# Layer 3's expert feed-forward in lanes of 32 rows, four experts to a round, with biases by a one-hot product, and one register load for all lanes

## The reference

```python
def _L3_ffn_ref(x, Wg, W1, b1, W2, b2):
    ...
    probs = jax.nn.softmax(logits, axis=-1)
    top1_val = probs.max(axis=-1).reshape(bt)
    top1_idx = probs.argmax(axis=-1).reshape(bt)
    masked = jnp.where(top1_idx[None, :] == jnp.arange(n)[:, None], top1_val[None, :], -jnp.inf)
    vals, idx = jax.lax.top_k(masked, cap)
    ...
    h = jax.nn.gelu(jnp.einsum('ncd,ndh->nch', xe, W1) + b1[:, None, :])
    out = jnp.einsum('nch,nhd->ncd', h, W2) + b2[:, None, :]
    ...  # tokens that were not kept stay as they are
```

## Time and profile before

| | |
|---|---|
| median of 3 runs | 1657.29 us (1657.05 to 1662.76) |
| the profiled execution | 1651.5 us, its span from first to last instruction 1649.8 us |
| TensorE busy over the span | 1462.4 us, 89% |
| VectorE, ScalarE, GpSimd busy | 60%, 40%, 26% |
| layer 0's lane rounds | from about 100 to 290 us of the span |
| layer 3's tiles | first up product at 1470.0, last `add_b2` at 1630.3 us |
| from there to the end | 19.5 us |

### The profile page before, as it was taken

How to read it: one execution, slowest core, us unless ns; L and a number is a source line. 1 busy time by engine, 2 the same in 40 slices (tenths; PEclk the granted TensorE clock), 3 DMA queues, 4 the chain that set the end, 5 groups by cost and what they waited for, 6 DMA issues and landing times. The chain is left out here.

```text
span 1649.8 us, 25908 instructions
## 1 busy us (share of the span) xinstructions
PE 1462.4 (89%) x8350; PEld 1109.7 (67%) x8350; DVE 983.9 (60%) x1754; ACT 657.0 (40%) x977; POOL 428.0 (26%) x366
## 2 busy tenths in 40 slices
PE   7997888765999999898999999999988999759994
PEld 5752333533787788687888888888877877536663
DVE  5666767335644364835777777775657433557665
ACT  3366767212233333324655555554333233211110
POOL 0602222000434410010333333332003443023331
PEclk9999999755999999999999999999998999859997
DMA  5348981652232240240220222210403332455743
GB/s 176 113 171 325 358 330 54 223 165 103 90 103 90 94 157 1 89 179 4 100 103 27 103 103 103 103 30 14 144 7 138 112 103 84 145 196 186 242 138 121
DMA packets 82919, 211.38 MB, mean 128 GB/s; under 512 B 10786, under 2 KB 57763, under 8 KB 74595
## 3 DMA queue, kind: packets, MB, share of 16 engines
q1 hardware_dynamic: 66944, 166.40, 28.2%
q0 software_dynamic: 15840, 43.27, 7.7%
q10 hardware_dynamic: 2, 0.00, 0.0%
HBM read 165.21 MB, written 44.43 MB: 127 GB/s over the span
## 5 line engine op out<-in xcount | busy, mean ns | idle before, releaser
L657 POOL DMA_INDIRECT results<-sb_big,sb_s_out_row x63 | 134.0, 2127 | 462.5 <-ACT sb_big L888 298.5
L962 DVE TENSOR_TENSOR sb_h_split<-sb_big,sb_h_split 128x2048 fp32r<-128x2048 f32 x78 | 178.5, 2289 | 87.1 <-ACT sb_h_split L957 87.1
L957 ACT CAST sb_h_split<-sb_big 128x2048 fp32r x78 | 146.6, 1903 | 34.1 <-issue 32.9
L853 PE MATMUL ps<-sb_big,sb_e_hT 128*128 x624 | 141.0, 379 | 1.1 <-DVE sb_e_hT L1010 1.1
L1102 DVE COPY sb_g_space<-sb_big 128x1024 f32 x168 | 107.9, 698 | 48.8 <-DMA sb_big<-in_l_routed 23.2
L320 PE MATMUL ps<-sb_h_split 128*128 128x512 f32 x312 | 133.3, 427 | 3.8 <-issue 2.8
L1102 ACT COPY sb_g_space<-sb_big 128x1024 f32 x120 | 118.5, 1046 | 40.7 <-DMA sb_big<-in_l_routed 21.7
L853 PEld LDWEIGHTS ps<-sb_big,sb_e_hT 128*128 128x128 f32 x624 | 118.2, 190 | 18.5 <-issue 1.3
L322 PE MATMUL ps<-sb_h_split 128*128 128x512 f32 x312 | 123.9, 397 | 0.0
L1503 POOL DMA_INDIRECT sorted_in<-sb_big,sb_p_slots x64 | 70.1, 1095 | 206.0 <-DVE sb_p_slots L1328 163.4
L321 PE MATMUL ps<-sb_h_split 128*128 128x512 f32 x312 | 123.4, 395 | 0.0
(11 more groups left out here) (450 smaller groups left out, 3180.5 us busy)
## 6 DMA issues: line engine op xcount, KB each, us to landing
sb_big<-in_l_routed SPq DMA_DIRECT2D x32, 1024.0 KB, 7.2
sb_big<-in_l2f_routed SPq DMA_DIRECT2D x8, 3072.0 KB, 10.6
sb_e_wring<-in_l_experts SPq DMA_DIRECT2D x16, 1408.0 KB, 6.8
sb_big<-in_l_routed SPq DMA_DIRECT2D x32, 512.0 KB, 7.4
sb_big<-results SPq DMA_DIRECT2D x32, 512.0 KB, 7.2
sb_big<-sorted_in SPq DMA_DIRECT2D x18, 512.0 KB, 4.2
by_token<-sb_big SPq DMA_DIRECT2D x12, 512.0 KB, 3.7
sorted_in<-sb_l1p_zero SPq DMA_DIRECT2D x2, 2048.0 KB, 9.6
```

Source lines behind the costliest of these rows:

```text
L657: pool.indirect_dma_start(out=results, out_offset=bass.IndirectOffsetOnAxis(ap=places.out_row[:, j:j + 1], axis=0), in_=self.tile(j), in_o ...
L853: last = pe.matmul(psum[:, 7, 0:D], self.hT[:, f // TPC, f % TPC * P:(f % TPC + 1) * P], self.weight(place, 2 * KD * self.F + f * D, D), s ...
L957: act.copy(self.own[part][:, 0, :], self.raw(e, part)).then_inc(self.own_high[part], 1)
L962: dve.tensor_tensor(self.own[part][:, 1, :], self.raw(e, part), self.own[part][:, 0, :], ALU.subtract).then_inc(self.own_low[part], 1)
```

## The change

Layer 3's feed-forward goes over to lanes. An expert gets units of 32 rows, so the most there can be are 4 * 16 + 15 = 79 units, in 20 rounds of four (`ROUNDS3`). With these inputs 72 of the 80 lanes hold tokens. A round does the following:

- ScalarE and VectorE copy two lanes' `W1` each to `own_up` (`fill_up`), and the four lanes' `W2` to `own_down` (`fill_down`: in even rounds three by ScalarE and one by VectorE, in odd ones two each). Both places hold one round, so a fill waits for the product of the round before.
- TensorE first multiplies a one-hot matrix `which` (16 experts x 128 rows, made once from the lanes' experts) with the biases of all experts, as a high and a low part in the type fp32r, and adds the lanes' products on top in the same bank (`add_bias`, `up_product`, `down_product`). ScalarE's gelu reads that bank, and ScalarE writes the down product's result (`result`). `add_b1` and `add_b2` are gone.
- TensorE reads no registers. ScalarE and VectorE read the round's four experts with one register load of four values.
- The 26 bits are spread over 20 rounds: one in an odd round and two in an even one (`tally_at`). `rank_even`, `choose_kept` and all of `add_dropped` come behind the last round.
- An expert's weights are 1 MB in two loads of 512 KB, each with a ring of four.

Layer 0's `experts_of` also loads all four numbers at once, on both engines. The diff, cut (removed lines that stand in the print above are mostly left out, and so are the waits and names that repeat):

```diff
+ROUNDS3 = -(-(LANES0 * NT + E3 - 1) // LANES0)
...
             def experts_of(self, eng, r, lanes):
-                return {g: eng.value_load(self.tile_expert[0:1, r * self.lanes + g:r * self.lanes + g + 1],
-                                          min_val=0, max_val=self.NE - 1) for g in lanes}
+                _, found = nc.values_load_multi_w_load_instructions(
+                    self.tile_expert[0:1, r * self.lanes:(r + 1) * self.lanes], engines=[eng.engine],
+                    min_val=0, max_val=self.NE - 1)
+                return dict(enumerate(found))
...
+            tally_at, n = {}, 0
+            for r in range(1, rounds):
+                for spot in range(2 - r % 2):
+                    if n <= TOP_BIT:
+                        tally_at[r, spot] = n
+                        n += 1
...
+                places = Slots("s3", own, route, runs0[:, 0:E, :], rounds, big[:, EXTRA:EXTRA + NT * D], None, LANES)
...
+                own_up = big[:, FCOL2:FCOL2 + LANES * UP].rearrange("p (g n) -> p g n", g=LANES)
+                own_down = big[:, EXTRA:EXTRA + LANES * DOWN].rearrange("p (g n) -> p g n", g=LANES)
+                ring_up = sb("e3_ring_up", [P, LANES, UP], on=own)
+                ring_down = sb("e3_ring_down", [P, LANES, DOWN], on=own)
+                bias = sb("e3_bias", [E, FU + D], on=own)
+                bias_high, bias_low = (sb("e3_" + n, [E, FU + D], F32R, on=own) for n in ("bias_high", "bias_low"))
+                expert_wide = sb("e3_expert_wide", [P, E], on=own)
+                which = sb("e3_which", [E, rounds * LANES, W], F32R, on=own)
...
+                def load_up(sp, e):
+                    if e >= 2:
+                        sp.wait_ge(up_in[e % 2], 16 * (e // 2) + e % 2)
+                    if e >= LANES:
+                        wait_last_round(sp, e - LANES, act_up, dve_up)
+                    sp.dma_start(ring_up[:, e % LANES, :], a["l3_experts"][e][:, 0:UP]).then_inc(up_in[e % 2], 16)
...
+                        for e in range(E + LANES - 1):
+                            if e < E:
+                                load_up(sp, e)
+                            if e >= LANES - 1:
+                                load_down(sp, e - LANES + 1)
+                            if e == LANES - 1:
+                                places.wait_known(sp)
...
+                        def tell_experts():
+                            pe.wait_ge(widened, 1)
+                            pe.matmul(psum[0:E, 5, 0:rounds * LANES], expert_wide[:], ident[:, 0:rounds * LANES],
+                                      start=True, stop=True).then_inc(told, 1)
+                        def add_bias(to, r, lo, n):
+                            lanes = which[:, r * LANES:(r + 1) * LANES, :].rearrange("e g w -> e (g w)")
+                            pe.matmul(to, lanes, bias_high[:, lo:lo + n], start=True, stop=False)
+                            pe.matmul(to, lanes, bias_low[:, lo:lo + n], start=False, stop=False)
+                        def up_product(r):
+                            if r >= 2:
+                                pe.wait_ge(raw, r - 1)
+                            add_bias(psum[:, r % 2, :], r, 0, FU)
+                            pe.wait_ge(rows_c, r + 1)
+                            pe.wait_ge(act_up, r + 1)
+                            pe.wait_ge(dve_up, r + 1)
                             for k in range(KD):
+                                for g in range(LANES):
+                                    lo = k * P + g * W
+                                    last = pe.matmul(psum[g * W:(g + 1) * W, r % 2, :], rT[:, r % 2, lo:lo + W],
+                                                     own_up[:, g, k * FU:(k + 1) * FU], start=False, stop=(k == KD - 1))
...
+                            pe.wait_ge(chosen, 1 if r == 0 else 2)
+                            up_product(r)
+                            if (r, 0) in tally_at:
+                                sum_tally(tally_at[r, 0])
+                            if r >= 1:
+                                turn_hidden(r - 1)
+                            if r + 1 < rounds:
+                                turn_rows(r + 1)
+                            if r >= 1:
+                                down_product(r - 1)
+                            if (r, 1) in tally_at:
+                                sum_tally(tally_at[r, 1])
+                        turn_hidden(rounds - 1)
+                        down_product(rounds - 1)
+                        sum_surely()
...
+                            wait_landed(act, down_in, experts[3])
+                            for g in range(1 + r % 2, LANES):
+                                last = act.copy(own_down[:, g, :], from_ring(ring_down, experts[g]))
...
+                        for r in range(rounds):
+                            now = experts
+                            if r + 1 < rounds:
+                                experts = experts_of(act, r + 1)
+                                fill_up(r + 1, experts)
+                                turned_rows(r + 1)
+                            act.wait_ge(up, r + 1)
+                            if r >= 2:
+                                act.wait_ge(hid_t, r - 1)
+                            act.activation(h[:, r % 2, :], psum[:, r % 2, :], ACT.Gelu_apprx_tanh).then_inc(raw, 1)
+                            if r >= 1:
+                                result(r - 1)
+                            if r == 0:
+                                act.wait_ge(places.traced, 1)
+                            fill_down(r, now)
+                        result(rounds - 1)
...
+                        def fill_up(r, experts):
+                            if r >= 1:
+                                dve.wait_ge(up, r)
+                            wait_landed(dve, up_in, experts[1])
+                            for g in (0, 1):
+                                last = dve.tensor_copy(own_up[:, g, :], from_ring(ring_up, experts[g]))
+                            last.then_inc(dve_up, 1)
+                        def fill_down(r, experts):
+                            if r >= 1:
+                                dve.wait_ge(down, r)
+                            wait_landed(dve, down_in, experts[r % 2])
+                            for g in range(1 + r % 2):
+                                last = dve.tensor_copy(own_down[:, g, :], from_ring(ring_down, experts[g]))
...
+                            told_rows = psum[0:E, 5, lo:hi].unsqueeze(2).to_broadcast([E, hi - lo, W])
+                            dve.tensor_scalar(which[:, lo:hi, :], told_rows, tile_rows[0:E, 0:1], None, ALU.is_equal
+                                              ).then_inc(chosen, 1)
...
+                        dve.tensor_tensor(bias_low[:], bias[:], bias_high[:], ALU.subtract).then_inc(bias_l, 1)
+                        choose_lanes(0, 0, LANES)
+                        experts = experts_of(dve, 0)
+                        fill_up(0, experts)
+                        choose_lanes(1, LANES, rounds * LANES)
+                        fill_down(0, experts)
...
+                        for r in range(rounds):
+                            now = experts
+                            if r >= 1:
+                                turned_hidden(r - 1)
+                            if r + 1 < rounds:
+                                experts = experts_of(dve, r + 1)
+                                fill_up(r + 1, experts)
+                            if (r, 0) in tally_at:
+                                try_bit(tally_at[r, 0] + 1)
+                            if r >= 1:
+                                fill_down(r, now)
+                            if (r, 1) in tally_at:
+                                try_bit(tally_at[r, 1] + 1)
+                        turned_hidden(rounds - 1)
+                        rank_even()
+                        choose_kept()
+                        add_dropped(0, NT)
```

227 lines of the change are left out of this document (102 added, 125 removed).

## The result

| | before | after |
|---|---|---|
| median of 8 runs | 1657.36 us (1653.24 to 1662.76) | 1665.60 us (1664.81 to 1668.77) |
| the profiled execution | 1651.5 us, span 1649.8 | 1665.1 us, span 1663.4 |
| TensorE, VectorE, ScalarE busy | 89%, 60%, 40% | 87%, 60%, 45% |
| layer 3's part, from the gate's product (L336) to the end | 210.8 us | 216.1 us |

The change makes the kernel slower, by 8.2 us or 0.5% by the two medians. The ratio of all executions is 1.0061, with a 95% interval of 1.0048 to 1.0075, which is 10 us. The forecast was no change.

A forecast was written before the change was run, and what follows sets the result against it. The prediction took TensorE to bound layer 3's tiles before and a chain through VectorE the new rounds. Layer 3 +1.3, layer 0 -4 and clock +2 made about -1 us, rounded to no change: 1657 us, range 1641 to 1677.

The forecast's parts named there:

- the chain through VectorE: Layer 3's rounds: VectorE's copy, load, fills and bits with TensorE's hand-overs set 15.7 us per two rounds, 7.85 a round.
- rival 4: Layer 3: full-width bias matmuls keep lanes from running beside each other, raising TensorE's 5.2 us; chance 0.04, shared with anything else slow.
- rival 3: Layer 3's register load costs like four single ones, 2.1 us: +0.9 in each of 19 rounds, 1672 us; chance 0.06.
- first up product, against that of before: Start of layer 3's loop: about 0.6 us later, for one more operation, low biases, a lane choice and a fill ahead.
- first two rounds: Layer 3's first two rounds run at the lower clock and take 15.2 us.
- eight pairs, chain alone: Layer 3's middle rounds: eight pairs of an even and an odd round at 15.7 us each, 126 us.
- drops of the clock: TensorE in layer 3: occasional drops after even rounds' gaps of about 2.3 us, two at 1 us each, +2.
- nineteenth round: Layer 3's nineteenth round takes 6.4 us, its bit being the last and half a one.
- last up product to the final additions: Layer 3's end, 1618 to 1639.0 us: last products, ranking, choosing and 16 `add_dropped` of 6.6 us in all.
- from there to the end: Final additions to the kernel's end: stores no longer decide, and the 0.2 us once waited there is saved.
- rival 1: Layer 3: gaps halve TensorE's clock again and again, a pair grows from 15.7 to 17.5 us, 1673 us; chance 0.23.
- Layer 0: Layer 0's lane rounds: shorter register loads give -2 in the last six rounds, -2 under the saturated DMA queue, sum -4.

The follow-up runs named there:

- The filler: Changed kernel plus 18 transposes of 128x128, result unread, before the second sum of each even round in layer 3; 0.9963 of the kernel before.
- layer 0 alone: Kernel before with only the change's layer 0 part, the lanes' experts read by one register load of four; 0.9985, on another chip 1.0000.
- the first group: Runs on one chip beside the kernel before: layer 0's part only 0.9985, layer 3's part only 1.0031, changed kernel with one bit 0.9837, with gap transposes 0.9963.
- the second group: Another chip: changed kernel 1.0063; with four single register loads 1.0261; with gap transposes plus rows off first 1.0012, or plus transposes ahead of first rounds 1.0017.

## Why the prediction was wrong

**The mechanism was right.** The two waits for weights are gone, TensorE no longer bounds the rounds, and the chain through VectorE gives the gain back. The up products alternate by 8.9 and 6.2 us (forecast 9 and 6.8), the undisturbed pair is 15.05 us (15.7), VectorE is idle 1.3 us ahead of the fills (1.0), TensorE 2.3 to 2.5 us ahead of each second sum (2.3). Without the bits the rounds are the 6 us that were named as their sign. Four lanes' products take 1.92 us, so rival 4 is out. The bias products take some 1.1 us a round (0.70 forecast); those of the up product, 0.66 for 0.46, are on the chain. The load of four with its arithmetic is 1.45 us of VectorE's queue (1.1 to 1.2 forecast, and just under the 1.5 that was named as rival 3's sign), and four single loads came to 1.0 us a round more than that, so rival 3 is out too.

**The sum for layer 3, term by term**, in the first trace of after against the forecast, in us:

| term | forecast | measured |
|---|---|---|
| first up product, against that of before | +0.6 | -0.1 |
| first two rounds | 15.2 | 18.3 |
| eight pairs, chain alone | 126 | 120.4 |
| drops of the clock | 2 | 8.9 |
| nineteenth round | 6.4 | 6.2 |
| last up product to the final additions | 21.0 | 19.85 |
| from there to the end | 12.0 | 11.4 |

Layer 3's part came out at +5.2 us against +3.3 with the clock. That these are near each other is luck: the clock was 6.9 us too low and the first two rounds 3.1, and the chain was 5.6 too high, the end 1.7 and the start 0.7.

**The step that failed** is "Two drops at 1 us each: +2". There were six, at 1.5 us each: 8.9 us. The two rows that the prediction had, a gap of 2.15 us that kept the clock and one of 3.19 that lost it, left gaps of 2.3 to 2.5 us open, and it took "occasional" out of that. In the seven traces of kernels with such gaps 44 of 56 were followed by a slow up product, six to seven of eight in each. This was rival 1 at some two thirds of its price. A disturbed pair takes 16.1 to 16.8 us, not 17.5 (the one right behind the long second round aside); only once in each of three traces is it 17.7, where the low clock set in late and lasted through the down product. Two rows, one on either side of the gap's length, did not support a chance as low as 0.23. The Trainium skill, "TensorE: Matmul & The Clock Gate", section "A second HAM failure mode: psum-queue depth-cycling", which was cited beside that rival, says of another kernel that frequent short idles make the clock oscillate, and the trace agrees (six of eight gaps). The filler gave the whole term back, some 9 us.

**What was not in the sum** is the second round: it took 9.4 to 12.1 us in place of 8.2 in all but one of the traces with ten gathers ahead on three of the four chips. What TensorE did behind the idle stretch then ran at the lower clock too. That is 2.9 us in the first trace (11.10 in place of 8.2), and 3.7, with 2.0 in the round behind it, in the worst. That GpSimd's gathers are the cause was shown on one chip, where three gathers ahead gave 7.75 and 7.57 us.

**What it was laid on.** The sum was made against one execution, and its layer 3 part (210.8 us) was the longest of the four traces that there are now of the old one (203.9, 206.6, 208.5). The new one's six are 213.9 to 222.1, 217.6 on average against 207.5. So layer 3 is 10 us slower in the mean of these few executions, between the 5.1 and 11.6 us where it ran alone. The trace with 203.9 us shows what made the first one long: its first three tiles take 14.3 us in place of 17.9, since TensorE's clock rises after the first, and waits for weights lengthen the tiles by 1.7 us in place of 4.2. Both were taken as what the old kernel costs.

**Layer 0**: forecast -4, measured -2.5 on one chip and 0.0, with 2.6 to either side, on another. The last rounds gave 1.6 us of the 2 forecast for them: three, not six, stood at 6.5 us and went to 6.13 to 6.16, and one went from 5.9 to 5.3. Where the DMA queue is saturated the trace of after is 0.7 us ahead by 252 us; the 2 us taken for it didn't come.

Together: layer 3 +10 and layer 0 between 0 and -2.5 make 7.5 to 10, where 8.2 by the medians and 10 by the ratio were measured. In the distance to the forecast the mis-sized clock is the largest single term that made it too low. The second round, the baseline and layer 0 add to it, and the chain and the end, which were priced too high, take a good part of that back.

## What to carry to other kernels

When work moves off the bounding engine, price the idle gaps that it opens on TensorE as clock, not only as idle time: gaps of 2.4 us cost 1.5 us each in three cases of four here, and dummy transposes took that cost away. Put register work ahead of the semaphore wait at which its engine stands anyway; that one line was worth 10 to 15 us here, about what the whole change had cost. And take the baseline of a sum from more than one trace: two readings of the same stage of the same kernel differed by 7 us.

## What was not expected of the hardware

- On three of four chips TensorE takes some ten instructions between 1284 and 1300 us with gaps of up to 2.3 us between them, always in the same stage of the program, with 7 to 8 us lost. No kernel here changes that code. GpSimd issues indirect DMAs one behind the other there (1.28 us apart), as it does in layer 3's second round, where fewer gathers removed the delay. But it issues them in the same way in the traces that have no hole (the first of before, and that of layer 0 alone in the first group). So the indirect DMAs by themselves don't make the hole; whether they are a part of its cause was not tried, and why one chip shows neither delay is open. The length of the second round also moved with the kernel on one and the same chip (11.1, 9.8, 9.4 and 8.4 us in the second group), which is open too.
- A register load of four values takes VectorE 0.35 us, and some 0.275 us follow for each value (0.18 of arithmetic and the gaps around it): 1.45 us, where one value is 0.31 + 0.19.
- The same kernel differs by 11 us between chips (the kernel before: medians 1647.2 to 1658.6 us in the groups), so only kernels beside each other compare.
